# Where the tensors of a tuned attention block lie in SBUF, modulo 512 bytes

## The reference

```
t1  = layer_norm(x, g1, be1)
att = softmax((t1 Wq' + bq)(t1 Wk' + bk)' / 4 + (1 - mask) * -1e9) (t1 Wv' + bv)     # per head
x   = x + att Wo' + bo
x   = x + memory Wg' + bg
t2  = layer_norm(x, g2, be2)
out = x + relu(t2 W1' + b1) W2' + b2
```

## The kernel before, in words

| kind | loaded | streamed | matmuls of 256 columns in a group |
|---|---|---|---|
| q, k (`which`) | `wq`, `wk` | `xT` | 12 + 12 |
| v | `xT` | `wv` | 12 |
| projection | `attnT`, `memT` | `wo`, `wg` | 12 + 12 |
| up (line 826) | `w1` | `zT` | 48 |
| down (line 965) | `hT` | `w2` | 48 |
| scores (line 844) | `q_stack` | `k_stack` | 16 |

## Time and profile before

### The profile page before, as it was taken

One profiled execution on the slowest core, in us unless ns is written; L12 is line 12 of the kernel. 1 busy time (PEld: TensorE's weight loads), 2 busy tenths in 40 slices (PEclk: granted clock), 3 DMA queues, 4 the chain that ended last, 5 costly groups with the idle time before them and its releaser, 6 DMA issues.

```text
span 1825.4 us, 53743 instructions
## 1 busy us (share of the span) xinstructions
PE 1783.9 (98%) x17972; PEld 1756.9 (96%) x17972; DVE 1351.8 (74%) x6810; ACT 1465.5 (80%) x5577; POOL 869.5 (48%) x907
## 2 busy tenths in 40 slices
PE   6799999999999999999999999999999999999997
PEld 5699999999999999999999999999999999999997
DVE  6677777777777777777777777777777777777762
ACT  4788888888887887887887887887887887887882
POOL 2254454454454454444444444444444444444454
PEclk7899999999999999999999999999999999999999
DMA  6665665665765765755755755755755755755730
GB/s 163 94 97 97 113 96 97 114 95 97 116 94 97 117 93 97 118 92 95 121 90 94 122 90 95 122 88 97 123 87 98 122 87 99 121 87 99 112 70 18
DMA packets 148931, 183.66 MB, mean 101 GB/s; under 512 B 14768, under 2 KB 99120, under 8 KB 148656
## 3 DMA queue, kind: packets, MB, share of 16 engines
q1 hardware_dynamic: 148656, 180.23, 59.3%
HBM read 62.73 MB, written 16.78 MB: 44 GB/s over the span
## 4 chain that ended last, share of the span: by engine, by line
PE 95%; ACT 1%; issue 0%; DMA 0%; DVE 0%; SPq 0%; ACTq 0%
PE ffn_ps L793 14%; PE ffn_ps L795 13%; PE ffn_ps L794 13%; PE turn_ps L858 12%; PE work_ps L793 9%; PE work_ps L795 8%; PE work_ps L794 8%; PE score_ps L844 7%; PE value_ps L884 6%; PE work_ps L810 3%; PE turn_ps L868 2%; ACT scores L366 1%; DMA k_stack<-k_hi 0%; ACT hid L409 0%; SPq L317 0%
## 5 line engine op out<-in xcount | busy, mean ns | idle before, releaser
L366 ACT ACTIVATE scores<-scores,row_min 128x128 f32<-128x128 f32 x2048 | 795.6, 400 | 2.6 <-DVE row_min L599 1.7
L719 POOL TENSOR_TENSOR hT_lo<-hid,hT_hi 128x512 fp32r<-128x512 f32 x256 | 356.5, 1392 | 575.2 <-DVE hT_hi L629 575.2
L376 ACT ACTIVATE probs<-turn_ps 128x512 f32<-128x512 f32 x512 | 302.8, 592 | 241.0 <-PE turn_ps L858 241.0
L599 DVE CUSTOM_DVE_ANT_0 scores<-score_ps,mask_bias 128x128 f32<-128x128 f32 x2048 | 470.9, 286 | 1.8 <-issue 1.8
L366 ACT ACTIVATION_READ_ACCUMULATOR scores<-scores,row_min 128x1 f32 x2048 | 406.6, 199 | 0.0
L858 PE MATMUL turn_ps<-ident,scores 128*128 128x128 f32 x2048 | 308.3, 273 | 3.3 <-ACT probs L376 3.2
L793 PE MATMUL ffn_ps<-zT_hi,w_lo 128*128 128x256 f32 x1024 | 305.1, 298 | 5.0 <-ACT hid L409 4.2
L793 PE MATMUL ffn_ps<-w_hi,hT_lo 128*128 128x256 f32 x1024 | 304.6, 297 | 2.4 <-ACT hid L409 2.4
L795 PE MATMUL ffn_ps<-w_hi,hT_hi 128*128 128x256 f32 x1024 | 289.2, 282 | 0.0
L795 PE MATMUL ffn_ps<-zT_hi,w_hi 128*128 128x256 f32 x1024 | 289.1, 282 | 0.0
L794 PE MATMUL ffn_ps<-zT_lo,w_hi 128*128 128x256 f32 x1024 | 288.8, 282 | 0.0
(11 more groups left out here) (113 smaller groups left out, 4279.7 us busy)
## 6 DMA issues: line engine op xcount, KB each, us to landing
q_stack<-q_hi SPq DMA_DIRECT2D x128, 256.0 KB, 6.9
k_stack<-k_hi SPq DMA_DIRECT2D x256, 128.0 KB, 6.4
x_in<-x_dram SPq DMA_DIRECT2D x64, 256.0 KB, 2.8
mem_in<-memory_dram SPq DMA_DIRECT2D x64, 256.0 KB, 6.9
x_res<-x_dram SPq DMA_DIRECT2D x64, 256.0 KB, 6.9
q_stack<-q_lo SPq DMA_DIRECT2D x64, 256.0 KB, 4.2
k_stack<-k_lo SPq DMA_DIRECT2D x128, 128.0 KB, 6.2
out_dram<-y SPq DMA_DIRECT2D x64, 256.0 KB, 2.1
```

Of the source, the lines that this page charges most:

```text
L366: last = act.activation(exps, exps, ACT.Exp, bias=row_min[:, k, h:h + 1], scale=-1.0, accum_out=row_sum[:, k, h:h + 1])
L376: act.activation(probs[:, k, :], turn_ps[k % 2][:, :], ACT.Copy).then_inc(probs_copied, 1)
L599: last = dve.tensor_tensor_reduce(out=scores[:, slot(i, t), h, :], in0=score_ps[t % 2][:, h * S:(h + 1) * S], in1=mask_bias[:, b, :], scal ...
L719: pool.tensor_tensor(halves[1], src, halves[0], ALU.subtract).then_inc(done, 1)
```

## The change

Only the order of the `sb` calls changes. The list of instructions, their operands by name and their order are the same; their addresses differ.

```diff
+        weight("q", KT * D)
+        weight("k", KT * D)
+        row_min, row_sum = sb("row_min", [P, CHUNKS, CH]), sb("row_sum", [P, CHUNKS, CH])
+        one = sb("one", [P, H])
+        zT = [sb("zT_hi", [P, KT, ROWS], F32R), sb("zT_lo", [P, KT, ROWS], F32R)]
+        k_stack = [sb(f"k_stack{n}", [P, CPB, 2, KT * GB, S], F32R) for n in range(2)]
+        stats1 = sb("stats1", [P, GB, 6])
+        q_stack = [sb(f"q_stack{n}", [P, CPB, KT, ROWS], F32R) for n in range(2)]
+        for n in "vog":
+            weight(n, KT * D)
+        weight("1", KT * FF)
+        weight("2", FT * D)
...
         hid = sb("hid", [P, 2, 2, ROWS])
+        y = sb("y", [P, GB, D])
+
+        stats2 = sb("stats2", [P, GB, 6])
+        xT = [sb("xT_hi", [P, KT, ROWS], F32R), sb("xT_lo", [P, KT, ROWS], F32R)]
+        attnT = [sb("attnT_hi", [P, KT, ROWS], F32R), sb("attnT_lo", [P, KT, ROWS], F32R)]
+        memT = [sb("memT_hi", [P, KT, ROWS], F32R), sb("memT_lo", [P, KT, ROWS], F32R)]
         hT = [sb("hT_hi", [P, FT, ROWS], F32R), sb("hT_lo", [P, FT, ROWS], F32R)]
-        y = sb("y", [P, GB, D])
```

More of the change, by code:

```diff
@@ L102, in sem, with weight @@
             return ctx.enter_context(nc.semaphore(name))
[L105 to L110, removed]
         weights = {}
-        for n, cols in (("q", KT * D), ("k", KT * D), ("v", KT * D), ("o", KT * D), ("g", KT * D),
-                        ("1", KT * FF), ("2", FT * D)):
+        def weight(n, cols):
             weights[n] = (sb(f"w{n}_hi", [P, cols], F32R), sb(f"w{n}_lo", [P, cols], F32R))
+        weight("q", KT * D)
[10 more added lines that the diff above has]
+        weight("2", FT * D)
         def tiles(n, k):
@@ L120, in xattn_block @@
         w1, w2 = tiles("1", KT), tiles("2", FT)
+        ident = sb("ident", [P, P])
+        row = sb("row", [P, 4, D])
+        bvw, bow, bgw, b2w = (row[:, n, :] for n in range(4))
         x_in = sb("x_in", [P, GB, D])
         xhat = sb("xhat", [P, GB, D])
-        xT = [sb("xT_hi", [P, KT, ROWS], F32R), sb("xT_lo", [P, KT, ROWS], F32R)]
         q = [sb("q_hi", [P, KT, ROWS], F32R), sb("q_lo", [P, KT, ROWS], F32R)]
         kk = [sb("k_hi", [P, KT, ROWS], F32R), sb("k_lo", [P, KT, ROWS], F32R)]
-        q_stack = [sb(f"q_stack{n}", [P, CPB, KT, ROWS], F32R) for n in range(2)]
-        k_stack = [sb(f"k_stack{n}", [P, CPB, 2, KT * GB, S], F32R) for n in range(2)]
         v_pad = [sb(f"v_pad{n}", [P, GB, H, 2 * HD]) for n in range(2)]
@@ L141, in xattn_block @@
         attn = sb("attn", [P, KT, ROWS])
-        attnT = [sb("attnT_hi", [P, KT, ROWS], F32R), sb("attnT_lo", [P, KT, ROWS], F32R)]
         mem_in = sb("mem_in", [P, KT, ROWS])
-        memT = [sb("memT_hi", [P, KT, ROWS], F32R), sb("memT_lo", [P, KT, ROWS], F32R)]
         x_res = sb("x_res", [P, GB, D])
@@ L147, in xattn_block @@
         xhat2 = sb("xhat2", [P, GB, D])
-        zT = [sb("zT_hi", [P, KT, ROWS], F32R), sb("zT_lo", [P, KT, ROWS], F32R)]
         resid_b2 = sb("resid_b2", [P, GB, D])
         hid = sb("hid", [P, 2, 2, ROWS])
+        y = sb("y", [P, GB, D])
[3 more added lines that the diff above has]
+        memT = [sb("memT_hi", [P, KT, ROWS], F32R), sb("memT_lo", [P, KT, ROWS], F32R)]
         hT = [sb("hT_hi", [P, FT, ROWS], F32R), sb("hT_lo", [P, FT, ROWS], F32R)]
-        y = sb("y", [P, GB, D])
         vector_cols, at = {}, 0
@@ L162, in xattn_block @@
         bqc, bkc = qk_bias[:, 0:KT], qk_bias[:, KT:2 * KT]
-        stats1, mv1 = sb("stats1", [P, GB, 6]), sb("mv1", [P, GB, 2])
+        sum_inv = sb("sum_inv", [P, GB, KT, CPB, 2])
+        mv1, mv2 = sb("mv1", [P, GB, 2]), sb("mv2", [P, GB, 2])
         var1, var2 = sb("var1", [P, GB]), sb("var2", [P, GB])
         carrier = sb("carrier", [P, CHUNKS])
-        stats2, mv2 = sb("stats2", [P, GB, 6]), sb("mv2", [P, GB, 2])
         rstd1, rstd2 = sb("rstd1", [P, GB]), sb("rstd2", [P, GB])
-        one = sb("one", [P, H])
         eps, minus_half = sb("eps", [P, GB]), sb("minus_half", [P, GB])
```

## The result

| | before | changed |
|---|---|---|
| median | 1826.17 us (4 runs) | 1808.92 us (1808.71 to 1810.33, 4 runs) |
| ratio | | 0.9906, 95% interval 0.9889 to 0.9924 |
| profiled execution, span | 1827.06, 1825.4 us | 1810.33, 1808.7 us |

The change takes off 17 us, 0.9%. Forecast were 35. The direction held, and 1808.92 us lies inside the stated range; the size is half of what was forecast.

A forecast was written before the change was run, and what follows sets the result against it. The prediction took TensorE's queue of matmuls to bound the kernel. Products were to gain 44 us less 8 already had, all other terms 0, so 1827.06 - 36 = 1791 us, range 1712 to 1843.

The forecast's parts named there:

- What bounds the kernel: Whole kernel: TensorE's matmul queue, 27.45 us a group; PE could gain 4.7 us a group before ScalarE binds.
- The products: All six kinds of 256-column products, 11,008 matmuls: distance falls from 120 to 116 ns, 36 us net.
- Case A: Products: part of the excess goes, distance 114 to 118 ns, time 1791 us (1769 to 1813); chance 0.34.
- the 8 us: Hidden layer's 6,144 loads average 190.7 and not 192 ns, so 8 us of the gain counted as already had.
- The transient behind a transpose: Products right behind a transpose: three distances of 117 ns, then 120; taken as sign of a collision depending on relative position.
- A sign that the prediction named: Profile after the change: product kinds should agree at one offset; otherwise the 64 bytes are not the variable that counts.
- Transfers. Cost 0.: Transfers filling q_stack and k_stack: PE waited twice, 9.1 us in all; even a tenth more is under 1 us.
- Transposes and values: Both operands stay at 0; about 20 borders with products a group, 4 us in all at 3 ns each; taken as 0.
- ScalarE, VectorE, GpSimd: Same tensors at other addresses, covered by 4.7 and 6.6 us idle a group; cost 0, busy times within 1%.
- B: Products: all of the excess goes, distance 109 ns, 113 us off, time 1714 us; chance 0.27.
- C: Products: nothing changes, the 13 ns being a path limit independent of addresses; 120 ns, 1827 us; chance 0.21.
- D: Products: slower, the stream having to pass the load's place inside each product; +16 us, 1843 us; chance 0.18.

The follow-up runs named there:

- e9: The kernel before, all operands level, with mem_in and x_res transfers moved in SP's queue and k's high part sent without awaiting the low; 1826.36 us, ratio 0.9997.
- e5: The changed kernel with mem_in and x_res transfers moved in SP's queue and k's high part sent without awaiting the low; 1788.57 us, ratio 0.9797.
- e1: The changed kernel with mem_in's transfers issued ahead of q_stack's and x_res's behind x_in's in SP's queue; 1802.43 us, ratio 0.9866.
- e2: The kernel before with only the mem_in and x_res transfers moved in SP's queue; 1827.65 us, ratio 1.0002.
- e6: The kernel before, SP's queue unchanged, with only the hidden layer's two kinds streaming 64 bytes below the load, other kinds level; 1805.84 us, ratio 0.9885.

## Why the prediction was wrong in its size

**What bounds the kernel: right for before, incomplete for after.** PE's queue set the end. That ScalarE's 22.75 us a group would bind next was wrong: `k_stack` did, with 0.57 us in hand a group in the median. It was not in the list of waits, because what is early leaves no row there. Its slack could have been read: six issues of 0.6 us, a landing in 6.4 us, against the start of the scores.

**The products: right in kind, close in size partly by luck.** Forecast was 116 ns and a net gain of 36 us. The mean fell to 115.4, and with the wait gone the layout gave 37.8 us (e9 to e5). Case A held: part of the excess over 109 ns went, in all six kinds. The sum behind the 36 us was less right than its result. It counted all 172 products of a group at 4 ns and took off 8 us as already had, which leaves 3.3 ns each. In the traces about 142 of them fell by some 4.2 ns, which makes 0.6 us a group and 38 us in all; the first product of a stretch, the last before a transpose and the scores gained about 2 ns or nothing. And the 8 us came from the loads' mean duration, where the distances before (119.6 and not 120) show 5. Too many products and too small a gain of each nearly cancel. The value of 116 was chosen between a row and a middle, as the prediction says, and not derived. Its bound of 109 ns rests on transposes that stream 128 columns and not 256; that their floor is 106.7 ns as well stands in no row, but the trace of before bears it out, where they take 213 ns at a granted clock of 0.50.

The transient behind a transpose (117 ns, then 120) was a useful lead: it showed that the distance can differ with all addresses alike, as the stretches that settle at 113 or 118 with the same addresses do.

**A sign that the prediction named and that came.** "The kinds should agree, as they have one offset now; if they don't, the 64 bytes are not the variable that counts." They didn't: 113.3 to 118 ns. By the table the offset does count, since 0 and 256 give 119.6 and -64 gives 115.4. But it isn't alone: at -64 two distances are open to a stretch, and the offset doesn't say which.

**The step that failed: "Transfers. Cost 0."** I argued that PE waited for `k_stack` only twice and that even a tenth more would be under 1 us. But PE became faster by 0.6 us a group while the chain of transfers did not, and `k_stack` had been only 0.57 us early. Cost of that term: 18.5 us by the trace, and 20.4 us by the medians of the changed kernel and e5, half of the gain. e1 and e5 took it away in two steps (10.5 us left, then 0), and e2 and e9 show that there was nothing to take away before. 36 - 18.5 = 17.5 us is close to the measured 17.2. "Even a tenth more is under 1 us" failed in itself too: it reckoned with the total of two waits, and the chain became 0.5 us longer in every group, some 0.4 us of it with the addresses (e6).

**Transposes and values: right within their bound.** A transpose is at 109 ns in both. From the last transpose to the second product behind it, it is 232.3 ns against 229.9 before, 2.4 ns more, some 8 times a group, 1.2 us in all, inside the 4 us allowed.

**ScalarE, VectorE, GpSimd: right.** Busy 1461.4, 1357.3 and 868.4 us, within 0.5% of the earlier trace rows.

**The rivals.** B (109 ns) happened at no offset; 113.3 is the least mean that a kind reached. C is refuted: the same instructions took 119.6, 118.6, 117.7 or 115.4 ns by the operands' addresses alone. So what the prediction took from the Trainium skill ("TensorE: Matmul & The Clock Gate", section "Step-by-step: what each phase is for"), that a load takes no read bandwidth from the running matmul and the sum would be zero, gave the wrong time for this kernel. That the load is what disturbs the stream is still argued and not shown, as no run had products without a load beside them. The other statement that it took from the Trainium skill, in "SBUF — State Buffer", section "SBUF: two separate sides", that PE never waits on anyone, stands there among rules on engines that share a port; no run here shows PE waiting for another engine's access, so they neither confirm nor refute it. And the 262 cycles that the prediction quotes from the Trainium skill ("TensorE: Matmul & The Clock Gate", section "Back-to-back issue gap") are given there for the isolated matmul, while for pairs of load and matmul the same section says that both set the spacing; so the 120 ns don't contradict it, and it doesn't make 11 ns recoverable. D occurred at none of the seven other offsets. My argument against B, that every distance occurs once in each product, holds only in part: it fits that no offset reached 109 ns, but it does not explain why one offset is better than the others.

Open is what the 256 bytes and the point at -64 are physically. The runs show a pattern in addresses, not its cause. Offsets finer than 32 bytes were not tried, nor different ones for different kinds beyond e6, nor level operands at another place than 0.

## What to carry to other kernels

When a change makes the bounding engine faster, go through everything that it needs per round and work out how early each arrives now: a wait of zero can be 0.5 us from binding, and the list of waits never shows it. Here two moves in a queue, worth nothing before, were worth 20 us after. And where matmuls come back to back, compare their distance with columns over clock: an excess that is constant to the nanosecond at full clock and absent at half clock is worth an experiment with addresses, since it costs no instruction.

## What the runs showed of the hardware that was not expected

- The mean distance of fp32r products of 256 columns, each loading 128, went with where the streamed operand starts against the loaded one: 119.6 ns level and at 256, 117.7 at +64 and 117.8 at -192, 115.4 at -64, 118.1 to 118.6 at -32, -96 and -128.
- At -64 a stretch of products settles at 113 or at 118 ns and keeps it (478 and 260 of 836 stretches in the changed kernel). With the same addresses the same stretch does the one in some groups and the other in others: q 23 and 38 times.
- First issue to last landing of the six transfers of `k_stack` rose from 10.5 to 11.0 us in the changed kernel; in e6, as fast and with `k_stack` at 0 modulo 512, it was 10.6 us.
